# Graph attention: subtracting the shifts and taking the exponentials in three operations a block in place of five

## The chip, the cores and the metric

The kernel runs on one core of one Trainium2 chip. Times are device microseconds (us) of one execution of the whole program; the time before is the median of three runs. The engines are named as the profile names them: PE (TensorE, with PEld for its weight loads), DVE (VectorE), ACT (ScalarE), POOL (GpSimd) and SP (SyncE, which here only issues DMAs).

## The reference, cut to what matters

Four graph layers stand one behind the other, each behind a layer norm and with a residual. The change touches only the last, an attention over edges in which every edge has its own 16 x 16 weights for the message and for the score:

```python
w_m = (efeat @ W_msg + b_msg).reshape(E, in_f, -1)
w_a = (efeat @ W_attn + b_attn).reshape(E, in_f, -1)
h_src = feat[src][:, :, None]
e1 = w_m * h_src
e2 = w_a * h_src
seg_max = jax.ops.segment_max(e2, dst, num_segments=N)
ex = jnp.exp(e2 - seg_max[dst])
denom = jax.ops.segment_sum(ex, dst, num_segments=N)
attn = ex / denom[dst]
ft = jax.ops.segment_sum(e1 * attn, dst, num_segments=N)
return ft.sum(axis=1)
```

There are 3125 nodes and 103125 edges (sorted by their target). In the kernel a running shift, which is at least as large as the scores that it covers, stands for `seg_max`.

## The kernel before, in words

The function `attention_edges` walks over the edges in 44 blocks. A block has 5 groups, and a group has 4 slots of 128 edges (one edge a partition). For each slot a tile `e[:, slot, :]` of 128 x 512 float32 holds the 256 scores e2 and the 256 messages e1 of each edge, in alternating runs of 16. Two blocks are in flight, in the two buffers `e0` and `e1` (index `u`, the other one is `w` or `1 - u`).

For a block, PE multiplies the edge features by the weights (L1724, `product`, tile `wps` in PSUM). What it makes is multiplied by the features of the source node, `hs`, which POOL gathers (L1700, 20 gathers a block). Twelve slots are multiplied by DVE, in three operations of four slots (L1830, the calls `next_block(0)`, `(1)` and `(2)`), and eight by ACT, with 16 small operations a slot (L1793): slots 4, 5, 6 before the exponentials (EARLY), slot 7 behind them (LATE1), and slots 12 to 15 last (LATE3). Then DVE takes maxima over the slots (L1850 and L1852, `largest`, in two steps; the second covers groups 3 and 4 and waits for ACT's last slot), carries them along the five groups (L1859, `up`, and L1864, `down`), makes `scale` (L1881, `rescale`), and subtracts the shift of each group from its scores (L1877, `subtract`). ACT takes the exponential of `scale` (L1799) and of the scores of each group (L1803, `exponentials`). One block later DVE multiplies the messages by the exponentials (L1895, `weigh`), and PE sums the four slots of groups 0 to 3 (L1746, `summed`, tile `slot_sums`); group 4 is summed on DVE (L1904 and L1909). DVE adds the sums up along the groups (L1930 for group 0, L1932 for the others, `accumulate`).

The order on each engine is the order in which the code is written; semaphores stand between the engines, and no scheduler moves anything. On DVE the order of a block around the change is, in `block_step`: `rescale`, `subtract` of group 4, `next_block(0)` (the first of the three multiplications of the next block), `subtract` of groups 3, 2, 1, 0, `accumulate` of group 2, `next_block(1)`, and so on. On ACT it is: EARLY of the next block, the exponential of `scale`, those of groups 4, 3, 2, 1, 0, LATE1 and LATE3 of the next block. Each exponential waits for its own subtraction on the semaphore `a_sub`. PE may refill the four PSUM banks that DVE reads once DVE's multiplication has read them (`a_read_v`), so its products of slots 8 to 11 wait for `next_block(0)`, and those of slots 16 to 19 for `next_block(1)`. ACT has two banks of its own.

Of the kernel before, what the change touches and what calls it, by code (L numbers as in the profile page):

```python
# [106 lines left out]
def bc(ap, axis, n):  # L107

    shape = list(ap.shape)
    shape.insert(axis, n)  # L110
    return ap.unsqueeze(axis).broadcast_to(shape)
# [1470 lines left out]
def attention_edges(nc, io, keep, d, sem, marks, lastrow):  # L1582
# [17 lines left out]
    SUM_READ = (3, 4, 6, 7)  # L1600
    SUM_DONE = (2, 2, 3, 4)
    NM = 2
    assert BG == 5 and SLOTS == 4 and sorted(ORDER) == list(range(BLK))
    with ExitStack() as ctx:
        def sb(name, shape, dt=F32):
# [43 lines left out]
        with nc.Block() as block:  # L1649
# [134 lines left out]
            @block.scalar  # L1784
            def _(act):
                def multiply(u, b, steps):

                    for s in steps:
                        act.wait_ge(a_mult, b * BLK + made(s))
                        bank = VBANKS + BYACT.index(s) % 2  # L1790
                        for f in range(F):
                            at = slice(f * 2 * F, (f + 1) * 2 * F)
                            ins = nc.scalar.mul(e[u][:, s, at], wps[:, bank, at], hs[u][:, s, f:f + 1])  # L1793
                        ins.then_inc(a_read_s, 1)

                def exponentials(u, b):

                    act.wait_ge(a_sub, b * (BG + 1) + 1)
                    nc.scalar.activation(scale[u][:, :], scale[u][:, :], ACT.Exp).then_inc(a_exp, 1)  # L1799
                    for n, g in enumerate(reversed(range(BG))):  # L1800
                        act.wait_ge(a_sub, b * (BG + 1) + (n + 2))
                        e2 = all_e2(u, g, g + 1)[:, 0, :, :]
                        nc.scalar.activation(e2, e2, ACT.Exp).then_inc(a_exp, 1)  # L1803

                act.sem_inc(a_read_s, NS)
                act.wait_ge(a_gather[0], GM)
                multiply(0, 0, BYACT)

                def turn(u, b, gathered):
                    act.wait_ge(a_gather[1 - u], gathered)  # L1810
                    act.wait_ge(a_sum, b * BYPE + 1)
                    multiply(1 - u, b + 1, EARLY)
                    exponentials(u, b)
                    multiply(1 - u, b + 1, LATE1)
                    act.wait_ge(a_sum, b * BYPE + 4)
                    multiply(1 - u, b + 1, LATE3)

                with act.Fori(0, BLOCKS // 2 - 1) as i:
                    turn(0, i * 2, i * GM + GM)
                    turn(1, i * 2 + 1, i * GM + 2 * GM)  # L1820
                turn(0, BLOCKS - 2, BLOCKS // 2 * GM)
                exponentials(1, BLOCKS - 1)

            @block.vector
            def _(dve):
# [45 lines left out]
                    down(u, 1).then_inc(a_shift, 1)  # L1871
                    dve.wait_ge(a_shift, b + 1)

                def subtract(u, g):
                    e2 = e[u][:, g * SLOTS:(g + 1) * SLOTS, :].rearrange("p c (i a o) -> p c i a o", a=2, o=F)[
                        :, :, :, 0, :]
                    nc.vector.tensor_tensor(e2, e2, bc(shift(u, g), 1, SLOTS), ALU.subtract).then_inc(a_sub, 1)  # L1877

                def rescale(u):

# [8 lines left out]

                def weigh(v, u, b):  # L1890

                    dve.wait_ge(a_exp, (b + 1) * (BG + 1))
                    for g in range(BG):
                        pair = e[u][:, g * SLOTS:(g + 1) * SLOTS, :].rearrange("p c (i a o) -> p (c i) a o", a=2, o=F)
                        ins = nc.vector.tensor_tensor(pair[:, :, 1, :], pair[:, :, 0, :], pair[:, :, 1, :], ALU.mult)  # L1895
# [59 lines left out]
                    v.wait(up(v, 0, g))  # L1955
                downs(v, 0, 0)
                rescale(0)
                for g in reversed(range(BG)):
                    subtract(0, g)
                dve.wait_ge(a_gather[1], GM)  # L1960
                for n in range(NV):
                    multiply(1, 1, n)
# [1 line left out]
                def block_step(v, u, b, i, more=True):  # L1964
# [32 lines left out]
                        if more:  # L1997
                            multiply(w, b + 1, n)

                    subtract(u, 4)  # L2000
                    next_block(0)
                    for g in reversed(range(4)):
                        subtract(u, g)
                    accumulate(v, w, b - 1, 2)
                    next_block(1)
                    dve.wait_ge(a_halved, b + 1)
# [258 lines left out]
```

## Time and profile before

| | |
|---|---|
| median of 3 runs | 3073.29 us (3070.06 to 3075.64) |
| profiled execution | 3085.54 us, its span 3083.7 us |
| granted TensorE clock, mean over the span | 0.81 of full speed |
| busy share of the span | PE 74%, DVE 71%, ACT 56%, POOL 46% |
| DVE in the attention stage (1500 to 2900 us) | 1315.67 of 1400 us |
| L1877, subtractions | 220 operations of 128 x 1024, 1215 ns each |
| L1803, exponentials | 220 operations of 128 x 1024, 1107 ns each (median 1057) |

The page gives shares over the whole program. The attention stage is its second half, from about 1390 to 2990 us, and everything that follows is read from that stage: the timeline of each engine through two or three neighbouring blocks, and the groups of instructions and waits in the window from 1500 to 2900 us, which holds 40 of the 44 blocks. In a timeline row the first number is the start, the second the time from the start of the first to the end of the last instruction of the row, and what stands in square brackets is the idle time before it with what ended it.

### The profile page before, as it was taken

Reading aid. Unit: us, or ns where it says so; the run is one execution under the profiler, and the core shown is the slowest. Engines: PE = TensorE matmul, PEld = TensorE weight load, DVE = VectorE, ACT = ScalarE, POOL = GpSimd, SP = SyncE. Lnnn points to the kernel's source line nnn. Section 1 sums busy time; section 2 is a strip of 40 time slices with the busy share of each in tenths; the row PEclk is TensorE's granted clock in tenths of the full one; section 3 lists DMA queues with packets and bytes.
Section 4 is the critical chain, followed back from the end, with each engine's and each line's share of the span. In section 5 each row is a group of like instructions: output and inputs, shape, how many; then the busy total and the mean of one; then the engine's idle time right before and its main releaser. Section 6 shows DMA issues by size and latency. Waiting matters only on the chain. (4 is left out here: it accounts for less than half of the span.)

```text
span 3083.7 us, 36754 instructions
## 1 busy us (share of the span) xinstructions
PE 2284.5 (74%) x7875; PEld 981.3 (32%) x7876; DVE 2192.9 (71%) x3603; ACT 1740.0 (56%) x6804; POOL 1427.2 (46%) x1214
## 2 busy tenths in 40 slices
PE   0588887169755898844888888888888888888860
PEld 0244444024432454321222222332223222223320
DVE  7799996011332444114999999999999999999976
ACT  3377774000110111106888888888888888888833
POOL 6000002710357100025677777677776777777503
PEclk9699999578766899965788888888877888888885
DMA  2000001300254554110222222222222222222113
GB/s 61 7 0 0 0 0 27 107 25 1 73 181 145 145 170 145 60 20 17 69 65 73 65 73 74 69 65 73 65 82 69 65 73 65 82 69 65 65 68 91
DMA packets 122611, 205.66 MB, mean 67 GB/s; under 512 B 55749, under 2 KB 77142, under 8 KB 116574
## 3 DMA queue, kind: packets, MB, share of 16 engines
q1 hardware_dynamic: 81806, 165.79, 15.4%
q0 software_dynamic: 40656, 38.45, 6.6%
q14 instruction: 124, 1.02, 0.1%
q8 instruction: 25, 0.41, 0.1%
HBM read 75.99 MB, written 128.17 MB: 66 GB/s over the span
## 5 line engine op out<-in xcount | busy, mean ns | idle before, releaser
L1700 POOL DMA_INDIRECT hs<-h_table,gix x880 | 1103.4, 1254 | 454.7 <-issue 271.8
L1793 ACT ACTIVATE e<-wps,hs 128x32 f32<-128x32 f32 x5632 | 1034.1, 404 | 239.7 <-PE wps L1724 146.7
L1724 PE MATMUL wps<-w_edge,ef 18*128 18x512 f32 x1760 | 578.8, 708 | 314.6 <-ACT e L1793 152.7
L1746 PE MATMUL slot_sums<-e,ident 128*128 128x512 f32 x1408 | 766.2, 695 | 9.4 <-DVE e L1895 7.0
L1746 PEld LDWEIGHTS slot_sums<-e,ident 128*128 128x128 f32 x1408 | 298.9, 224 | 495.8 <-issue 468.3
L537 POOL DMA_INDIRECT got<-in_edge_rows,start x152 | 153.9, 1013 | 507.9 <-POOLq L449 420.1
L1724 PEld LDWEIGHTS wps<-w_edge,ef 18*128 18x128 f32 x1760 | 159.0, 200 | 691.1 <-ACT e L1793 302.4
L511 ACT CAST edges<-acc 128x400 f32 x600 | 295.4, 492 | 121.0 <-PE acc L498 94.8
L494 PE MATMUL acc<-q_hot,lo_hot 128*128 128x400 bf16 x1200 | 307.0, 338 | 54.4 <-DVE q_hot L468 52.2
L1830 DVE TENSOR_TENSOR e<-wps,hs 128x2048 f32<-128x2048 f32 x132 | 301.5, 2284 | 41.3 <-PE wps L1724 34.2
L468 DVE TENSOR_SCALAR q_hot<-qcol,qT 128x400 bf16<-128x400 bf16 x1200 | 290.3, 316 | 0.9 <-PE acc L498 0.8
L1877 DVE TENSOR_TENSOR e<-e,shifts 128x1024 f32<-128x1024 f32 x220 | 256.6, 1215 | 0.0
L1803 ACT ACTIVATE e<-e 128x1024 f32<-128x1024 f32 x220 | 241.6, 1107 | 25.2 <-issue 9.9
L1895 DVE TENSOR_TENSOR e<-e 128x1024 f32<-128x1024 f32 x220 | 253.4, 1218 | 0.0
L1253 PE MATMUL acc<-edges,msg_parts 128*128 128x448 bf16 x1050 | 225.3, 370 | 36.8 <-DMA msg_parts<-msg 27.9
L498 PE MATMUL acc<-edges,ident_b 128*128 x600 | 202.9, 338 | 0.0
L1281 ACT COPY efT<-tr 128x512 f32<-128x512 f32 x56 | 32.8, 586 | 277.9 <-PE tr L1262 161.4
L494 PEld LDWEIGHTS acc<-q_hot,lo_hot 128*128 128x128 bf16 x1200 | 130.9, 140 | 94.2 <-DVE q_hot L468 69.1
L1850 DVE TENSOR_TENSOR pairs<-e 128x1536 f32<-128x1536 f32 x88 | 130.9, 1488 | 31.0 <-ACT e L1793 30.9
L1253 PEld LDWEIGHTS acc<-edges,msg_parts 128*128 128x128 bf16 x1050 | 106.8, 102 | 134.3 <-DMA msg_parts<-msg 28.3
L829 ACT ACTIVATE agg<-acc 128x448 f32<-128x448 f32 (+1 forms) x15 | 7.4, 535 | 239.1 <-remote 130.3
L1302 DVE SCALAR_TENSOR_TENSOR src_order<-missing,got_order 128x16 int32 (+1 forms) x56 | 10.4, 185 | 175.5 <-DMA got_order<-edges_order 166.2
(362 smaller groups left out, 2167.2 us busy)
## 6 DMA issues: line engine op xcount, KB each, us to landing
rows_state<-states SPq DMA_DIRECT2D x44, 1280.0 KB
rows_shift<-shifts SPq DMA_DIRECT2D x44, 640.0 KB
got_order<-edges_order SPq DMA_DIRECT2D x56, 256.0 KB
ef_order<-efT SPq DMA_DIRECT2D x56, 256.0 KB
ef<-ef_order SPq DMA_DIRECT2D x44, 320.0 KB, 3.0
hs<-h_table,gix POOLq DMA_INDIRECT x880
edges_order<-got SPq DMA_DIRECT2D x38, 256.0 KB
msg<-m_parts SPq DMA_DIRECT2D x10, 480.0 KB
```

Of the source, the lines that this page charges most:

```text
L468: ins = nc.vector.tensor_scalar(q_hot[:, k % HOTS, s, :], qcol[:, :], qT[:, s, at], None, ALU.is_equal)
L494: nc.tensor.matmul(total, lo_hot[:, k // HOTS % 2, :, k % HOTS * 2 + s], q_hot[:, k % HOTS, s, :], start=(s == 0), stop=False)
L511: nc.scalar.copy(edges[:, :, bass.ds(s16, W)], acc[:, k % BANKS, 0:QW].rearrange("p (t w) -> p t w", w=W)).then_inc(taken, 1)
L1253: ins = nc.tensor.matmul(acc[:, at, 0:CW], parts[:, f, k, a, :], edges[:, k, at * CW:(at + 1) * CW], start=(n == 0), stop=(n == 3 * TILES ...
L1700: nc.gpsimd.indirect_dma_start(out=hs[u][:, s, :], out_offset=None, in_=d["h_table"], in_offset=bass.IndirectOffsetOnAxis(ap=gix[u][:, s:s ...
L1724: nc.tensor.matmul(wps[:, bank, :], ef[u][k:k + KM, g * P:(g + 1) * P], w[k:k + KM, :], start=True, stop=True).then_inc(a_mult, 1)
L1746: ins = nc.tensor.matmul(sums[:, g % 2, :], ident[:, :], e[u][:, g * SLOTS + c, :], start=(c == 0), stop=(c == SLOTS - 1))
L1793: ins = nc.scalar.mul(e[u][:, s, at], wps[:, bank, at], hs[u][:, s, f:f + 1])
L1803: nc.scalar.activation(e2, e2, ACT.Exp).then_inc(a_exp, 1)
L1830: nc.vector.tensor_tensor(e[u][:, s0:s1, :].rearrange("p s (i c) -> p (s i) c", c=2 * F), wps[:, 0:s1 - s0, :].rearrange("p s (i c) -> p ( ...
L1877: nc.vector.tensor_tensor(e2, e2, bc(shift(u, g), 1, SLOTS), ALU.subtract).then_inc(a_sub, 1)
L1895: ins = nc.vector.tensor_tensor(pair[:, :, 1, :], pair[:, :, 0, :], pair[:, :, 1, :], ALU.mult)
```

## The change

The scores of two groups are handled by one operation, where before each group had its own: groups 3 and 4, then groups 1 and 2, then group 0 alone. This holds for the subtraction on DVE and for the exponential on ACT. `next_block(0)` keeps its place behind the first subtraction, so it now stands behind that of groups 3 and 4. The semaphores count 4 steps a block in place of 6.

```diff
+    SPANS = ((3, 5), (1, 3), (0, 1))
+    NE = len(SPANS) + 1
...
-                    act.wait_ge(a_sub, b * (BG + 1) + 1)
+                    act.wait_ge(a_sub, b * NE + 1)
                     nc.scalar.activation(scale[u][:, :], scale[u][:, :], ACT.Exp).then_inc(a_exp, 1)
-                    for n, g in enumerate(reversed(range(BG))):
-                        act.wait_ge(a_sub, b * (BG + 1) + (n + 2))
-                        e2 = all_e2(u, g, g + 1)[:, 0, :, :]
+                    for n, (g0, g1) in enumerate(SPANS):
+                        act.wait_ge(a_sub, b * NE + (n + 2))
+                        e2 = all_e2(u, g0, g1)
                         nc.scalar.activation(e2, e2, ACT.Exp).then_inc(a_exp, 1)
...
-                def subtract(u, g):
-                    e2 = e[u][:, g * SLOTS:(g + 1) * SLOTS, :].rearrange("p c (i a o) -> p c i a o", a=2, o=F)[
-                        :, :, :, 0, :]
-                    nc.vector.tensor_tensor(e2, e2, bc(shift(u, g), 1, SLOTS), ALU.subtract).then_inc(a_sub, 1)
+                def subtract(u, g0, g1):
+                    e2 = e[u][:, g0 * SLOTS:g1 * SLOTS, :].rearrange(
+                        "p (g c) (i a o) -> p g c i a o", c=SLOTS, a=2, o=F)[:, :, :, :, 0, :]
+                    low = shifts[u][:, g0:g1, :].rearrange("p g (i o) -> p g i o", o=F)
+                    nc.vector.tensor_tensor(e2, e2, bc(low, 2, SLOTS), ALU.subtract).then_inc(a_sub, 1)
...
-                    dve.wait_ge(a_exp, (b + 1) * (BG + 1))
+                    dve.wait_ge(a_exp, (b + 1) * NE)
...
-                    subtract(u, 4)
+                    subtract(u, *SPANS[0])
                     next_block(0)
-                    for g in reversed(range(4)):
-                        subtract(u, g)
+                    for g0, g1 in SPANS[1:]:
+                        subtract(u, g0, g1)
                     accumulate(v, w, b - 1, 2)
                     next_block(1)
```

On DVE, in the loop, the stretch from `rescale` to `next_block(1)` stood so before (`e0` is the block whose scores are shifted, `e1` the next one; a row with "x4" is four instructions, 128x64x16 is one group's 1024 scores):

```order
L1881 SCALAR_TENSOR_TENSOR scale0<-shifts1,mk0,shifts0 128x256
L1994 ISA
L1877 TENSOR_TENSOR e0<-e0,shifts0 128x64x16
L1829 ISA
L1830 TENSOR_TENSOR e1<-wps,hs1 128x2048
L1877 TENSOR_TENSOR e0<-e0,shifts0 128x64x16 x4
L1924 REGISTER_ALU
L1928 REGISTER_ALU
L1932 SCALAR_TENSOR_TENSOR states1<-states1,mk1,slot_sums 128x512
L1829 REGISTER_ALU
L1830 TENSOR_TENSOR e1<-wps,hs1 128x2048
```

The same stretch of DVE with the change:

```order
L1884 SCALAR_TENSOR_TENSOR scale0<-shifts1,mk0,shifts0 128x256
L1997 ISA
L1880 TENSOR_TENSOR e0<-e0,shifts0 128x128x16
L1831 ISA
L1832 TENSOR_TENSOR e1<-wps,hs1 128x2048
L1880 TENSOR_TENSOR e0<-e0,shifts0 128x128x16
L1880 TENSOR_TENSOR e0<-e0,shifts0 128x64x16
L1927 REGISTER_ALU
L1931 REGISTER_ALU
L1935 SCALAR_TENSOR_TENSOR states1<-states1,mk1,slot_sums 128x512
L1831 REGISTER_ALU
L1832 TENSOR_TENSOR e1<-wps,hs1 128x2048
```

The multiplication of the next block stands behind two groups' subtraction in place of one group's, and the operation behind it covers two groups before it counts its semaphore.

On ACT, in the loop, the exponentials with the change (the last 16 multiplications of EARLY ahead of them, LATE1 behind; `e1` is shifted here, `e0` is the next block):

```order
L1795 ACTIVATE e0<-wps,hs0 128x32 x16
L1801 ACTIVATE scale1<-scale1 128x256
L1803 REGISTER_ALU
L1805 ACTIVATE e1<-e1 128x128x16
L1803 REGISTER_ALU
L1805 ACTIVATE e1<-e1 128x128x16
L1803 REGISTER_ALU
L1805 ACTIVATE e1<-e1 128x64x16
L1791 REGISTER_ALU
L1795 ACTIVATE e0<-wps,hs0 128x32 x16
```

Before, five rows `L1803 ACTIVATE e1<-e1 128x64x16` stood in the place of these three; nothing else moved on ACT, and PE, POOL and SP have the same instructions as before.

## Rows read from the trace of the kernel before

**Rows 1.** The page: busy tenths of DVE in 40 slices of the span.

```profile
DVE  7799996011332444114999999999999999999976
```

**Rows 2.** Groups by form, 1500 to 2900 us: xcount, busy us, mean ns, idle, releasers.

```profile
L1877 DVE TENSOR_TENSOR e<-e,shifts 128x1024 f32<-128x1024 f32 x200 | 233.4, 1215 | 0.0
L1803 ACT ACTIVATE e<-e 128x1024 f32<-128x1024 f32 x199 | 219.0, 1101 | 22.7 <-issue 9.5 <-DVE e L1877 3.7
L1850 DVE TENSOR_TENSOR pairs<-e 128x1024 f32<-128x1024 f32 x40 | 49.0, 1225 | 23.2 <-ACT e L1793 23.2
```

**Rows 3.** Timeline of DVE, blocks from 2000 to 2082 us.

```profile
2000.37 1.23 DVE L1850 TENSOR_TENSOR pairs<-e 128x1024 f32<-128x1024 f32 x1 [0.77 <-ACT e L1793]
...
2006.57 0.69 DVE L1930 TENSOR_TENSOR states<-states,slot_sums 128x512 f32<-128x512 f32 x1 [0.16 <-PE slot_sums L1746]
...
2010.45 1.21 DVE L1877 TENSOR_TENSOR e<-e,shifts 128x1024 f32<-128x1024 f32 x1
2011.59 2.28 DVE L1830 TENSOR_TENSOR e<-wps,hs 128x2048 f32<-128x2048 f32 x1
2013.79 4.62 DVE L1877 TENSOR_TENSOR e<-e,shifts 128x1024 f32<-128x1024 f32 x4
...
2021.78 0.74 DVE L1932 SCALAR_TENSOR_TENSOR states<-states,mk,slot_sums 128x512 f32<-128x512 f32 x1
...
2034.75 1.23 DVE L1850 TENSOR_TENSOR pairs<-e 128x1024 f32<-128x1024 f32 x1 [0.54 <-ACT e L1793]
...
2042.61 0.69 DVE L1930 TENSOR_TENSOR states<-states,slot_sums 128x512 f32<-128x512 f32 x1 [1.83 <-PE slot_sums L1746]
...
2057.81 0.74 DVE L1932 SCALAR_TENSOR_TENSOR states<-states,mk,slot_sums 128x512 f32<-128x512 f32 x1
```

**Rows 4.** Timeline of ACT, the same stretch.

```profile
2013.38 1.31 ACT L1803 ACTIVATE e<-e 128x1024 f32<-128x1024 f32 x1
2015.03 4.46 ACT L1803 ACTIVATE e<-e 128x1024 f32<-128x1024 f32 x4 [0.34 <-issue]
2019.40 7.23 ACT L1793 ACTIVATE e<-wps,hs 128x32 f32<-128x32 f32 x40
...
2027.65 7.07 ACT L1793 ACTIVATE e<-wps,hs 128x32 f32<-128x32 f32 x39 [0.42 <-issue]
```

**Rows 5.** Line L1803: ns min/median/max; timeline of ACT, the first block's exponentials.

```profile
L1803 ACT ACTIVATE e<-e x220: 1052/1057/1439, 1446.4 to 2967.4; 128x1024 f32<-128x1024 f32 x110
...
1446.40 5.22 ACT L1803 ACTIVATE e<-e 128x1024 f32<-128x1024 f32 x5
```

**Rows 6.** The page, groups: two ACT copies of 400 and 512 columns.

```profile
L511 ACT CAST edges<-acc 128x400 f32 x600 | 295.4, 492 | 121.0 <-PE acc L498 94.8
L1281 ACT COPY efT<-tr 128x512 f32<-128x512 f32 x56 | 32.8, 586 | 277.9 <-PE tr L1262 161.4
```

**Rows 7.** Timeline of PE, the same blocks as rows 3.

```profile
2013.92 1.14 PE L1724 MATMUL wps<-w_edge,ef 18*128 18x512 f32 x8 [0.78 <-issue]
2014.99 3.70 PE L1746 MATMUL slot_sums<-e,ident 128*128 128x512 f32 x8
...
2021.32 2.20 PE L1724 MATMUL wps<-w_edge,ef 18*128 18x512 f32 x10 [1.58 <-DVE e L1830]
...
2051.12 5.25 PE L1746 MATMUL slot_sums<-e,ident 128*128 128x512 f32 x8
```

**Rows 8.** Waits, 1500 to 2900 us: total us, times, longest.

```profile
POOL hs L1700 <- ACT e L1793: 161.4, 40, 5.8
DVE states L1930 <- PE slot_sums L1746: 34.2, 32, 2.0
DVE states L1930 <- DVE shifts L1859: 6.7, 8, 1.0
```

**Rows 9.** Stretches: length, busy us of PE, PEld, DVE, ACT, POOL, PEclk, DMA, GB/s.

```profile
2000.40:2006.60 6.20, 6.20 (x18) 2.25 (x20) 5.90 (x10) 4.25 (x17) 4.50 (x4) 1.00 0.07 6
2020.00:2034.70 14.70, 9.73 (x18) 3.11 (x19) 14.01 (x14) 13.97 (x78) 10.15 (x8) 0.62 0.36 117
```

More of the change, by code:

```diff
@@ L1957, in _ @@
                 rescale(0)
-                for g in reversed(range(BG)):
-                    subtract(0, g)
+                for g0, g1 in SPANS:
+                    subtract(0, g0, g1)
                 dve.wait_ge(a_gather[1], GM)
```

## The prediction

> **What bounds the kernel now.** I read the page first. Over the span no engine is full, but DVE's slices show a 9 in nearly every slice of the second half, the attention stage [rows 1]. The chain that ended last reaches back only some 50 us, into the output stage, and says nothing of the blocks. So I took the groups by form for 40 blocks, and then the timelines of DVE, ACT and PE through neighbouring blocks.
>
> The reader is to see that each block is closed by a ring through two engines. The second maximum, L1850, starts at 2000.37 and again at 2034.75 [rows 3]: 34.38 us. Take it apart:
> - from the maximum at 2000.37 to the first subtraction at 2010.45: 10.08 us of DVE work [rows 3];
> - from there to the second exponential at 2015.03: 4.58 us. Between them DVE does that subtraction, the multiplication of the next block and the second subtraction, which begins at 2013.79 and lasts 1.215 us [rows 2, 3], so it ends at 2015.00, and ACT starts 0.03 later. The profile calls ACT's 0.34 us of idle there "issue" [rows 4], but the times show what ended it;
> - from 2015.03 to the next multiplication on ACT at 2019.40: 4.37 us [rows 4];
> - from there ACT multiplies five slots, to 2027.65 + 7.07 = 2034.72: 15.32 us [rows 4];
> - 0.03 us to the maximum, which had waited 0.54 us for just this [rows 3].
>
> The sum is 34.38. Two waits tell that the ring holds everywhere: the second maximum waited for ACT 23.2 us in 40 blocks, 0.58 each [rows 2], and the exponentials stood idle 22.7 us in those blocks, 0.57 each, of which 0.34 is the case above. So what is done on DVE ahead of the second exponential is on the ring, and what DVE does behind it is not: it ends 0.58 us early. DVE's high share is no bound by itself.
>
> One more thing is to be seen in the four exponentials in a row. They take 4.46 us, 1.057 being the last one's own (the median of all [rows 5]), so they start (4.46 - 1.057)/3 = 1.135 us apart [rows 4]. The four subtractions take 4.62 us, which gives (4.62 - 1.215)/3 = 1.135 as well [rows 3]. ACT is paced by DVE. Left alone it is quicker: in the first block, where the subtractions had a lead, five exponentials take 5.22 us, about (5.22 - 1.43)/4 = 0.947 apart, if one record there, which overlaps what was ahead of it, is about as long as the longest of the line, 1.439 [rows 5]; at 5.22/5 each they are 1.044, still under 1.135.
>
> **The change part by part.**
>
> DVE. A subtraction of 1024 scores takes 1.215 us and the next starts after 1.135. One of 2048 has no row; the multiplication of 128 x 2048 lasts 2.28 us and the instruction behind it starts 2.20 us after it (2011.59 to 2013.79) [rows 3]. It reads PSUM and this one does not, so I bound it by the 1024 scores themselves: at most two of them back to back, 1.135 + 1.215 = 2.35, the next start after 2.27; at the other end 0.09 less than the row of 2048, 2.19 and 2.11, should it save twice as much against the two as that row does (0.07). I take the row of the same size, 2.28 and 2.20. A block saves 5 x 1.135 - (2 x 2.20 + 1.135) = 0.14 us on DVE. By itself this is worth nothing: it falls in the part that ends 0.58 us early.
>
> Now the order. Start from the first subtraction, 2010.45. With the change it covers groups 3 and 4, and the multiplication starts at 2012.65 (before 2011.59), the second subtraction, of groups 1 and 2, at 2014.85 and ends at 2014.85 + 2.28 = 2017.13. Before, ACT had its second piece of work at 2015.00. It now has more in its first piece, but not enough.
>
> ACT. What 1024 more columns cost in one exponential: two copies of 400 and 512 columns give (586 - 492)/112 = 0.84 ns a column [rows 6], 0.86 us. The other end is a whole further exponential as the first block spaces them, 0.947 us. I take 0.86, since the fixed part is paid once: 1.057 + 0.86 = 1.91 us. The first exponential starts at 2013.38 as before (it waits for ACT's own EARLY work, not for DVE: the subtraction is done at 2010.45 + 2.28 = 2012.73) and ends at 2013.38 + 1.31 + 0.86 = 2015.55. Then ACT waits for the second subtraction until 2017.16, that is 1.6 us in place of 0.34. The second exponential ends at 2019.07, the third (its scores are subtracted by 2017.05 + 1.215 = 2018.27, so it waits for nothing) 0.947 later, at 2020.02. Before, the last one ended at 2015.03 + 4.46 = 2019.49. So the five slots behind it start **0.53 us later**, and with them the next maximum. Bounds of this term: 0.35 (the subtraction at its lower end, 0.09 off both operations ahead of the second exponential) to 0.95 (both at their upper end, 0.14 on top, the exponential at 2.00, another 0.09, and the last one after 1.135 in place of 0.947, 0.19).
>
> What else moves. `next_block(0)` ends 1.06 us later, so PE's products of slots 8 to 11 start at 2014.98 in place of 2013.92, and the sums of group 3 behind them end at 2019.75 in place of 2018.69 [rows 7]. DVE needs them at 2021.78 [rows 3], ACT for slot 12 at about 2020.0 + 2.9 (a fifth of 15.3, roughly). In the neighbouring block the same sums took 5.25 us, to 2056.37 [rows 7]; 1.06 later is 2057.43, and DVE asks at 2057.81 - 0.14 = 2057.67. Covered, barely; and what is beyond it first eats DVE's lead, which grows to 0.58 + 0.53 + 0.14 = 1.25 us. If that cover were gone too, each us over costs one. `next_block(1)` comes 0.14 earlier. The weighing of the block waits for all exponentials, and stands some 5 us behind them on DVE. POOL's gathers wait for ACT's last slots, 161.4/40 = 4.0 us a block [rows 8], so they have room in a longer block. SP's queue and the DMAs are untouched.
>
> The sum. 42 blocks have the ring as drawn (44 less the first, whose exponentials start late behind ACT's own work and wait for nothing, and the last, which has no next block): 42 x 0.53 = 22.3 us. The first block gains perhaps 0.2, the last 0.1. Together **+22 us**. The profiled execution took 3085.5 us (span 3083.7), so one like it would take 3107.5. The median of the runs is 3073.3, 12 less; the difference is added to it: **3095 us**.
>
> **The rivals.**
>
> A. *Fewer fixed costs win.* The Trainium skill, "VectorE: DVE Perf Modes", section "The TRN2 errata — SBUF-src ops pay a fixed extra latency per instruction", says that a single large tile pays that latency once and many small ones pay it each time. The trace agrees as far as it shows a price (two spacings of 1.135 against one of 2.20 are 0.07 us apart), but has it in a place with slack. As a mechanism in rows: if the second exponential were not held, ACT would be through at 2015.55 + 1.80 + 0.947 = 2018.3, 1.2 us earlier than now, and DVE's lead of 0.58 + 0.14 = 0.72 would be the next limit: 42 x 0.72 = 30 us, 3043 us. For it speaks only that both engines save work; against it that the second subtraction would have to end at 2015.55 and not at 2017.13.
>
> B. *The clock of PE takes more.* DVE waits for the slot sums at L1930: 0.16 us in one block and 1.83 in the next [rows 3], (34.2 + 6.7)/40 = 1.02 on average [rows 8], and this wait is on the ring. The stretch ahead of it, in which PE makes single products and waits, has a granted clock of 0.62, a mixture of both levels (1.2 and 2.4 GHz), and where the clock is back at 1.00 the wait is the short one [rows 9]. The change makes the idle time ahead of slots 8 to 11 longer, 0.78 + 1.06 = 1.84 us, and the wait of PE for ACT behind slots 16 to 19 too. If this brought 1.83 us in each block: 42 x 0.81 = 34 us on top, 3129; half of it, 3112.
>
> The Trainium skill, "TensorE: Matmul & The Clock Gate", section "What's actually happening", has it that activity releases the throttle and the throttled state is the default. That is rival B's direction; no row here shows how a moved gap would be taken.
>
> C. *The clock of PE gives it back*, the side of no loss. The gap of 1.58 us ahead of slots 16 to 19 [rows 7] shrinks to about 1.58 - 1.06 - 0.14 = 0.4, so the sparse stretch that pulls the clock down begins later. If the fall came so late, or ended so early, that every block had the wait of 0.16, the ring would lose 0.86 a block, 36 us: 3095 - 36 = 3059. It decides from a gain of 0.53 a block, that is, once the mean wait falls from 1.02 to 0.5; half of it is 3077.
>
> D. *The change does less than it says*: operations of two groups that cost as much as two. Both engines would then save nothing, with the upper bound of the ring's term: 42 x 0.95 = 40 us, 3113.
>
> **How the numbers follow.** The forecast with its own range (0.35 to 0.7 a block and a wait within 0.2 of today's, 3080 to 3111): 0.60. A: 0.05. B: 0.17. C: 0.13. D: 0.05. About 0.2% (6 us) is what a measurement of this kernel can tell from no change. Faster than 3067: A and the far half of C, 0.08. Within: the near half of C and the lower edge of the forecast, 0.11. Slower than 3079: 0.81. The range to hold 8 in 10 leaves out A, the far half of C and the far half of B: 3072 to 3124.
>
> **What would show it.** In the profile after: the second exponential of a block starts 6.7 us behind the first subtraction, with 1.6 us of idle ahead of it; operations of 2.28 us on DVE and 1.91 us on ACT; the last exponential ends 9.57 us behind the first subtraction (9.04 before); DVE's wait ahead of the second maximum grows from 0.58 to some 1.25; L1930's wait is still near 1.0 (this decides between B, C and the forecast); a block like the one from 2000.37 to 2034.75 takes 34.9 us in place of 34.38. The forecast is wrong if the ring is not one: if DVE did not wait for ACT's last slot, or if the exponentials had no idle time before the second.

## The result, and the profile after

The change made the kernel slower by 3.0%: 3168.55 us, median of 6 runs (3162.42 to 3178.57), against 3077.89 for the kernel before on the same chip, a ratio of 1.0303 (95% interval 1.028 to 1.0326). The forecast was 3095, with a range of 3072 to 3124. Its direction was right, and its size a quarter of the truth: +22 us forecast, +91 us measured. The profiled execution took 3176.3 us with a span of 3174.5 us (before: 3083.7), so it can stand for the others; its mean granted clock is 0.817, as before (0.814).

All of it lies in the blocks. From the page after, the tenths of DVE, which answer to [rows 1], and those of the clock:

```profile
DVE  6899994021332451118898898888888898888876
PEclk9999998587876999757787887778887788788785
```

Where the row of before had a 9 in nearly every slice of the second half, there are now mostly 8s: DVE waits more. Groups by form, 1500 to 2960 us (busy us, mean ns | idle us ahead and its cause), which answer to [rows 2]:

```profile
L1880 DVE TENSOR_TENSOR e<-e,shifts 128x2048 f32<-128x2048 f32 x78 | 177.9, 2280 | 0.0
L1805 ACT ACTIVATE e<-e 128x2048 f32<-128x2048 f32 x78 | 158.4, 2031 | 64.2 <-DVE e L1880 64.2
L1852 DVE TENSOR_TENSOR pairs<-e 128x1024 f32<-128x1024 f32 x39 | 47.8, 1225 | 107.2 <-ACT e L1795 107.2
```

The wait ahead of the second exponential is there, 64.2/39 = 1.6 us a block. But the second maximum now waits 107.2/39 = 2.7 us for ACT, where 0.58 was the measured value before and 1.25 the forecast. Something holds ACT in its five slots behind the exponentials. Waits, 1500 to 2900 us (total us, times, longest), beside [rows 8]:

```profile
ACT e L1795 <- issue: 87.3, 176, 1.3
DVE states L1933 <- PE slot_sums L1748: 24.0, 28, 1.9
```

L1933 is the wait that was L1930 before. It has gone down from 34.2 us, not up. And ACT has 87.3 us of idle in its multiplications that no semaphore explains ("issue"). The same row in the trace of before:

```profile
ACT e L1793 <- issue: 26.8, 78, 0.5
```

To see where the time went I took each block apart at three points: M, the start of the second maximum; R, the start of the small rescaling right ahead of the first subtraction; and the end of the last exponential. All are starts and ends in the timelines; the values are means over 40 blocks, the third to the forty-second. "Low" is the time of a block in which the granted clock was under 1, "sums" the start and end of group 3's sums on PE behind R, "13 to 14" the time between the starts of these slots on ACT.

| kernel | block | M to R | R to last exp | five slots | low | sums | 13 to 14 |
|---|---|---|---|---|---|---|---|
| before | 35.25 | 10.53 | 9.45 | 15.28 | 12.5 | 4.99 to 9.19 | 4.03 |
| after | 37.62 | 10.24 | 9.98 | 17.40 | 14.8 | 6.33 to 11.62 | 5.63 |

The block is 2.37 us longer, and 40 x 2.37 = 95 us against 90.8 in the span. The forecast's term is the third column of times, R to the last exponential: +0.53. The next one, the five slots, carries the miss: +2.12 us, for work that is the same as before; 1.60 of it lies between the starts of slots 13 and 14.

Here are three blocks in a row, beginning (R) at 2038.44, 2073.24 and 2112.70. DVE, which answers to [rows 3]:

```profile
2028.15 1.22 DVE L1852 TENSOR_TENSOR pairs<-e 128x1024 f32<-128x1024 f32 x1 [1.64 <-ACT e L1795]
...
2038.84 2.28 DVE L1880 TENSOR_TENSOR e<-e,shifts 128x2048 f32<-128x2048 f32 x1
2041.04 2.28 DVE L1832 TENSOR_TENSOR e<-wps,hs 128x2048 f32<-128x2048 f32 x1
...
2053.97 5.76 DVE L1898 TENSOR_TENSOR e<-e 128x1024 f32<-128x1024 f32 x5
...
2063.82 1.23 DVE L1852 TENSOR_TENSOR pairs<-e 128x1024 f32<-128x1024 f32 x1 [1.36 <-ACT e L1795]
...
2089.06 5.79 DVE L1898 TENSOR_TENSOR e<-e 128x1024 f32<-128x1024 f32 x5
...
2101.62 1.23 DVE L1852 TENSOR_TENSOR pairs<-e 128x1024 f32<-128x1024 f32 x1 [4.04 <-ACT e L1795]
```

ACT, which answers to [rows 4]:

```profile
2045.56 2.86 ACT L1805 ACTIVATE e<-e 128x2048 f32<-128x2048 f32 x2 [1.64 <-DVE e L1880]
2048.32 6.49 ACT L1795 ACTIVATE e<-wps,hs 128x32 f32<-128x32 f32 x36
...
2083.13 6.35 ACT L1795 ACTIVATE e<-wps,hs 128x32 f32<-128x32 f32 x35
2089.94 0.29 ACT L1795 ACTIVATE e<-wps,hs 128x32 f32<-128x32 f32 x1 [0.46 <-issue]
2090.65 0.29 ACT L1795 ACTIVATE e<-wps,hs 128x32 f32<-128x32 f32 x1 [0.43 <-issue]
...
2093.49 0.47 ACT L1795 ACTIVATE e<-wps,hs 128x32 f32<-128x32 f32 x2 [1.11 <-issue]
...
2122.60 2.94 ACT L1795 ACTIVATE e<-wps,hs 128x32 f32<-128x32 f32 x16
2126.71 3.66 ACT L1795 ACTIVATE e<-wps,hs 128x32 f32<-128x32 f32 x20 [1.18 <-issue]
```

PE, which answers to [rows 7] (a matmul of the program is two instructions there, so the four products and the four sums have x8), and three stretches with their granted clock (the number behind POOL's), which answer to [rows 9]:

```profile
2043.38 1.14 PE L1726 MATMUL wps<-w_edge,ef 18*128 18x512 f32 x8 [1.84 <-DVE e L1832]
2044.45 3.70 PE L1748 MATMUL slot_sums<-e,ident 128*128 128x512 f32 x8
...
2078.19 1.14 PE L1726 MATMUL wps<-w_edge,ef 18*128 18x512 f32 x8 [1.93 <-DVE e L1832]
2079.26 5.40 PE L1748 MATMUL slot_sums<-e,ident 128*128 128x512 f32 x8
2084.59 2.65 PE L1726 MATMUL wps<-w_edge,ef 18*128 18x512 f32 x12
...
2117.66 2.09 PE L1726 MATMUL wps<-w_edge,ef 18*128 18x512 f32 x8 [1.84 <-DVE e L1832]
2119.68 5.95 PE L1748 MATMUL slot_sums<-e,ident 128*128 128x512 f32 x8
```

```profile
2044.40:2048.10 3.70, 3.70 (x13) 1.46 (x9) 3.70 (x4) 2.54 (x2) 3.09 (x3) 1.00 0.02 2
2079.20:2084.60 5.40, 5.40 (x14) 2.05 (x10) 5.40 (x5) 4.24 (x11) 4.49 (x4) 0.68 0.05 5
2119.60:2125.50 5.90, 5.90 (x12) 2.30 (x8) 4.80 (x5) 5.66 (x18) 4.68 (x5) 0.61 0.05 6
```

Read them together:

- In the first block all goes as the forecast had it. The second exponential starts at 2045.56, 6.72 us behind the first subtraction, with 1.64 us of idle; it and the third end at 2048.42, 9.58 us behind (forecast 9.57). The five slots take 2063.82 - 2048.42 = 15.40 us. PE stood idle 1.84 us for `next_block(0)` (0.78 before), but its clock held: 3.70 us for the sums.
- In the second and the third the clock is at its lower level for some 64% and 78% of the four sums (granted clocks of 0.68 and 0.61): they take 5.40 and 5.95 us. The four products ahead of them take 1.14 or 2.09 us.
- What follows is of two kinds. In the third block ACT, through with slot 7 at 2125.54, waits 1.18 us for slot 12, whose product is behind the sums. In the second the products of slots 16 to 19 come late, and `next_block(2)` and the weighing with them: the weighing starts at R + 15.82 (2089.06) against R + 15.53 (2053.97) in the first. And ACT then gets its multiplications slowly: from 2089.94 they start 0.72 us apart, where sixteen in a row take 2.94 us, 0.18 apart. This block lost some 3 us that way; its wait ahead of the second maximum is 4.04 us.

Of the 40 blocks, 6 are like the first (sums of 3.70 us, five slots of 15.42 on average), 21 like the second (5.40 and 17.76) and 13 like the third (5.70 to 6.03, and 17.72). A slow clock in these sums was no loss by itself: the kernel before has sums of 5.06 to 5.29 us in 13 of its 40 blocks, and the five slots take 15.25 us there. But they start at R + 5.07 on average and end by R + 10.4, where those of the second kind end at R + 11.4.

So what the forecast had left out seems to be the clock, but at another place and by another path than its rival B had it. The experiments test this.

### The profile page after: what moved, and what is told of

It reads as the page before. It is cut to its first block and busy times, and to the rows that moved or that the text cites. A ratio compares the mean times of both kernels' runs of the same rounds, so it can differ in the third digit from the quotient of the medians.

```text
span 3174.5 us, 36410 instructions
## 1 busy us (share of the span) xinstructions
PE 2277.0 (72%) x7875; PEld 988.7 (31%) x7876; DVE 2189.6 (69%) x3515; ACT 1726.8 (54%) x6716; POOL 1431.3 (45%) x1214
## 3 DMA queue, kind: packets, MB, share of 16 engines
q1 hardware_dynamic: 81806, 165.79, 14.8%
q14 instruction: 124, 1.02, 0.1%
## 5 line engine op out<-in xcount | busy, mean ns | idle before, releaser
L1726 PE MATMUL wps<-w_edge,ef 18*128 18x512 f32 x1760 | 547.3, 724 | 406.8 <-ACT e L1795 128.5
L1748 PE MATMUL slot_sums<-e,ident 128*128 128x512 f32 x1408 | 804.3, 725 | 9.4 <-DVE e L1898 6.8
L1748 PEld LDWEIGHTS slot_sums<-e,ident 128*128 128x128 f32 x1408 | 311.9, 233 | 530.6 <-issue 493.4
L1805 ACT ACTIVATE e<-e 128x2048 f32<-128x2048 f32 x132 | 220.1, 1704 | 71.5 <-DVE e L1880 71.5
L1880 DVE TENSOR_TENSOR e<-e,shifts 128x2048 f32<-128x2048 f32 x132 | 250.5, 1926 | 0.0
L1302 DVE SCALAR_TENSOR_TENSOR src_order<-missing,got_order 128x16 int32 (+1 forms) x56 | 10.4, 186 | 176.1 <-DMA got_order<-edges_order 169.0
```

Source lines behind the costliest of these rows:

```text
L1726: nc.tensor.matmul(wps[:, bank, :], ef[u][k:k + KM, g * P:(g + 1) * P], w[k:k + KM, :], start=True, stop=True).then_inc(a_mult, 1)
L1748: ins = nc.tensor.matmul(sums[:, g % 2, :], ident[:, :], e[u][:, g * SLOTS + c, :], start=(c == 0), stop=(c == SLOTS - 1))
L1880: nc.vector.tensor_tensor(e2, e2, bc(low, 2, SLOTS), ALU.subtract).then_inc(a_sub, 1)
```

## The experiments

Every time is a median, and its ratio is against runs of the kernel before taken beside it. That kernel's own median went from 3074 to 3081 us between sets, so a few us between two experiments of different sets say nothing. "Means" are those of the table above.

### Which part of the change costs it

The first set took the change apart: the multiplication behind two subtractions, with all operations one group each (e1); the exponentials alone in pairs (e2); the subtractions alone in pairs (e4). A fourth kernel asked whether the store of the states holds ACT back.

e1, the order alone, from the kernel before:

```
+                    subtract(u, 3)
                     next_block(0)
-                    for g in reversed(range(4)):
+                    for g in reversed(range(3)):
                         subtract(u, g)
```

> Five subtractions and five exponentials as before; only next_block(0) stands one subtraction later (behind groups 4 and 3), so it ends 1.13 us later, about as much as the changed kernel has it (1.06). Measured in the changed kernel: last exponential +0.53 us, the five slots behind it 15.28 -> 17.40 us a block (+2.1). Theory P (the late multiplication, through PE's products of slots 8 to 11 and the sums behind them, makes the +2.1): about 2 us a block more than before, 3078 + 85 = 3160 us. Theory S (the +2.1 is a stretch in which ACT and PE get their instructions slowly, which starts some 1.8 us behind the start of the state store and lasts longer when ACT's slots come 0.5 us later; the late multiplication has no part in it): the last exponential is still paced by the subtractions and ends where it did, 3078 to 3085 us.

Measured: 3170.15 us, ratio 1.0291 (1.0228 to 1.0353). The last exponential ends where it did before (9.45 us behind R), and no operation is wider, and yet a loss of the same size is here. The block is 37.53 us: the five slots take 16.89 us, M to R 11.19. The path is not quite that of the change. All 40 blocks of e1 are of the third kind (sums of 5.91 to 5.99 us): slot 12 starts 4.71 us behind slot 7, 2.72 before, and from slot 13 to 14 it is 3.68 us, with no slow stretch.

e2, the exponentials alone, from the kernel before:

```
-                    for n, g in enumerate(reversed(range(BG))):
-                        act.wait_ge(a_sub, b * (BG + 1) + (n + 2))
-                        e2 = all_e2(u, g, g + 1)[:, 0, :, :]
+                    for g0, g1 in ((3, 5), (1, 3), (0, 1)):
+                        act.wait_ge(a_sub, b * (BG + 1) + (BG + 1 - g0))
+                        e2 = all_e2(u, g0, g1)
...
```

> Exponentials over two groups at a time, subtractions one by one with next_block(0) in its old place. The second exponential has to wait for the third and fourth... by the spacing of 1.135 us the first (groups 3, 4) starts at 4.58 us behind the first subtraction, the second at 6.85, the last ends at 9.7 (9.04 before): +0.65 us a block on the ring, and PE is not delayed. Theory P: only that, 3078 + 27 = 3105 us, ACT's five slots still 15.3 us. Theory S: ACT's slots come 0.65 later, the slow stretch grows as in the changed kernel, 15.3 -> about 17, 3165 us.

Measured: 3104.46 us, ratio 1.01 (1.0061 to 1.014). The multiplication stands where it stood, and only the ring's term is left: the last exponential ends at R + 10.13 (9.45), the five slots take 15.33 us as before, the block 35.81.

e4, the subtractions in pairs, the exponentials one by one, from the kernel after:

```
-                    for n, (g0, g1) in enumerate(SPANS):
+                    for g, n in ((4, 0), (3, 0), (2, 1), (1, 1), (0, 2)):
...
-                        e2 = all_e2(u, g0, g1)
+                        e2 = all_e2(u, g, g + 1)
...
```

> Subtractions over two groups at a time with next_block(0) behind the first of them, exponentials one by one. Last exponential: the one of group 2 starts at 6.71 us behind the first subtraction, then two more at 0.947: ends at 9.66, +0.62 us a block. Both theories give about what the changed kernel takes, 3165 to 3175 us; if the length of the exponentials had a part in the slow stretch, it would differ.

Measured: 3174.99 us, ratio 1.0323 (1.0283 to 1.0364), a block of 37.71 us. Taking the exponentials apart again gives nothing back.

e5, the store of the states half a block later, from the kernel after:

```
+                        store_states(u, i * 2 + (u - 2))
...
-                        store_states(1 - u, i * 2 + (u - 1))
...
```

> The changed kernel with the store of a block's states (1280 KB) issued some 8 us later, behind the load of the next features, away from ACT's slots 12 to 15. Theory S: the slow stretch moves or goes, ACT's five slots fall towards 5 x 2.72 = 13.6 to 15.3 us, 3100 us or less. Theory P, and any theory in which the store has no part: unchanged, 3168 us.

Measured: 3145.38 us, ratio 1.0241 (1.0201 to 1.0281). Neither theory had this. The stretches of slow multiplications are there with no store beside them, so the store is not what makes them. It gave some 22 us back, measured against the kernel before of either set (the five slots take 16.48 us in place of 17.40), by what path stays open.

So the loss beyond the ring's term goes with the one thing that e1, e4 and the change share: `next_block(0)` a microsecond later.

### Is it the idle time of PE

e7 takes group 3's sums out of the way: they go ahead of the products that wait for `next_block(0)`.

```
+                    add(3)
                     for_dve(u, b, 1, NV + 1)
-                    add(3)
                     for_act(u, b, (12,))
```

e8 leaves the order, and fills PE's idle time ahead of these products with two matmuls whose result is thrown away:

```
+                    if before is not None:
+                        pe.wait_ge(a_weighed, before * BYPE + 4)
+                        pe.wait_ge(a_acc, before * BG + SUM_READ[3])
+                        for _ in range(2):
+                            nc.tensor.matmul(sums[:, 1, :], ident[:, :], e[u][:, 3 * SLOTS, :],
+                                             start=True, stop=True)
                     for_dve(u, b, 1, NV + 1)
```

> The changed kernel, but PE sums group 3 ahead of the products of slots 8 to 11, so it has 3.7 us of work while it would wait for next_block(0). In the changed kernel PE idles 1.84 us there (0.78 before), and the four products (2.09 us, 1.14 before) and the sums behind them (5.4 to 6 us, 3.7 before) run at the lower clock in most blocks. Theory C (the gap pulls the clock down, and what is late by it is the cost): sums of group 3 end near 5.8 us behind the scaling in each block, ACT's five slots fall back to 15.3 us, only the ring's 0.53 us a block is left, 3078 + 22 = 3100 us. Theory S (slow issue on ACT from its later place): ACT's slots stay at 17 us, 3165 us.

> The changed kernel with two more matmuls of 128 x 512 (about 0.93 us each at the higher clock) ahead of the wait for next_block(0); they write the bank that the sums of group 3 overwrite afterwards, and nothing else is moved. Theory C: PE has no gap, the clock stays up, the late products cost nothing by themselves, 3100 us. If the mere lateness by 1.06 us of the products and sums (and not the clock) is the cost, nothing changes, 3168 us.

Measured: e7 3081.68 us, ratio 1.0023 (1.0009 to 1.0038); e8 3096.3 us, ratio 1.0068 (1.0043 to 1.0093). e8 is the plainest of all tests: the same products, sums and operations as in the change, 1.98 us of extra work on PE, and 72 us less. Timeline of PE in e8:

```profile
2019.50 1.98 PE L1771 MATMUL slot_sums<-e,ident 128*128 128x512 f32 x4
2021.42 1.14 PE L1726 MATMUL wps<-w_edge,ef 18*128 18x512 f32 x8
2022.49 3.70 PE L1748 MATMUL slot_sums<-e,ident 128*128 128x512 f32 x8
```

There is no idle time ahead of the four products, and the sums take 3.70 us, in this block as in all 40. They still start at R + 6.03, so their later start alone costs nothing. The block is 35.67 us with five slots of 15.34, and the rest over the kernel before is the ring's: +0.42 a block, x 42 = 18 us. Against the kernel before of its own set (3075.5) e8 takes 21 us more; the forecast had 22. In e7 the sums run in the time in which PE had been idle (timeline of PE; waits of ACT):

```profile
2034.93 3.70 PE L1748 MATMUL slot_sums<-e,ident 128*128 128x512 f32 x8
2038.56 1.98 PE L1726 MATMUL wps<-w_edge,ef 18*128 18x512 f32 x10
```

```profile
ACT e L1795 <- issue: 12.4, 47, 0.4
```

It also shows that the amount of low clock does not tell the cost: e7 has as much of it as the change (14.8 us a block), but not over the sums of group 3, which take 3.70 us in all 40 blocks. ACT's unexplained idle falls from 87.3 to 12.4 us. That e7 even wins back most of the ring's 0.53 (its five slots take 15.00 us, 0.28 less than before, and M to R 10.26) I had not expected.

e9 is the control: the same edit as e7 on the kernel before.

> The kernel before with the same order on PE (sums of group 3 ahead of the products of slots 8 to 11), as a control for the two above. Theory C: the gap before was 0.78 us and pulled the clock down in one block of three at most, so little is to be had: 3065 to 3080 us. If the order alone is worth 2 us a block, it shows here too: below 3030 us.

Measured: 3077.67 us, ratio 1.0005 (0.9988 to 1.0023), nothing. In the kernel before, where PE idles 0.78 us, the order of these sums does not matter.

### Can the change be made to win

e10 is e7 with all three subtractions ahead of `next_block(0)`, so that no exponential waits.

```
-                    subtract(u, *SPANS[0])
-                    next_block(0)
-                    for g0, g1 in SPANS[1:]:
+                    for g0, g1 in SPANS:
                         subtract(u, g0, g1)
+                    next_block(0)
```

> Pairs of groups as in the changed kernel, but all three subtractions stand ahead of next_block(0), with the sums of group 3 first on PE. By the ring: exponentials start 2.93 us behind the first subtraction and are no longer held: 1.91 + 1.80 + 0.95, the last one ends at about 7.6 (9.04 before, 9.57 in the changed kernel), 1.4 us a block less than before; DVE's own work allows some 0.7 to 1.2 of it. 3078 - 42 x 0.9 = 3040 us, bounds 3010 and 3060. next_block(1) will wait some 0.5 us for PE's products of slots 8 to 11, and if this late next_block(0) pulls the clock down where it is needed, the gain is lost: 3100 us or more.

Measured: 3169.76 us, ratio 1.0312 (1.0283 to 1.0342), a miss of 130 us. The last exponential ends 1.23 us earlier than before (R + 8.22), where 1.4 was expected, and that is lost three times over: the five slots take 19.2 us. ACT, PE and DVE in one block of e10:

```profile
2019.68 6.04 ACT L1795 ACTIVATE e<-wps,hs 128x32 f32<-128x32 f32 x32
...
2029.87 2.60 ACT L1795 ACTIVATE e<-wps,hs 128x32 f32<-128x32 f32 x14 [4.15 <-PE wps L1726]
```

```profile
2023.76 3.79 PE L1726 MATMUL wps<-w_edge,ef 18*128 18x512 f32 x10 [1.65 <-issue]
2027.70 2.07 PE L1726 MATMUL wps<-w_edge,ef 18*128 18x512 f32 x2 [0.15 <-remote]
```

```profile
2027.70 2.29 DVE L1832 TENSOR_TENSOR e<-wps,hs 128x2048 f32<-128x2048 f32 x1 [1.95 <-PE wps L1726]
```

ACT, through with slots 7 and 12 at 2025.72, waits 4.15 us for slot 13. Its product stands on PE behind those of slots 16 to 19, which must wait until `next_block(1)` has read their banks, and the five run at the lower clock (3.79 us; five such products take 1.98 at the higher). I had looked at ACT's wait and not at what is queued ahead of it. This explains 1.8 us of the 4.15: by its row, whose end the profile models, the product of slot 13 is done at 2027.55, and ACT starts at 2029.87. DVE's `next_block(2)` also starts late, at 2027.70, where the products of slots 16 to 19 end at 2025.85 by their rows; over the blocks this difference is 1.8 us on average. What holds both up is not shown.

e11 fills PE's sparse stretch in the kernel before: one throw-away matmul ahead of the products of 16 to 19, two ahead of slot 14, one ahead of slot 15.

```
...
+                def fill(before, n):
+                    if before is None:
+                        return
+                    pe.wait_ge(a_acc, before * BG + (BG + 3))
+                    for _ in range(n):
+                        nc.tensor.matmul(sums[:, 0, :], ident[:, :], bc(ones[:, :], 1, 4), start=True, stop=True)
...
+                    fill(before, 1)
                     for_dve(u, b, 2, NV + 2)
-                    for_act(u, b, (13, 14, 15))
+                    for_act(u, b, (13,))
+                    fill(before, 2)
+                    for_act(u, b, (14,))
+                    fill(before, 1)
+                    for_act(u, b, (15,))
```

> The kernel before with matmuls on constants, whose results nobody reads, in the three places where PE waits late in a block: one ahead of the products of slots 16 to 19, two ahead of slot 14, one ahead of slot 15 (0.93 us each at the higher clock). Theory C (PE's waits late in a block pull the clock down over the sums of groups 1 and 0, and the wait at L1930, 1.02 us a block on average, is its price): the clock stays up, the wait falls to 0.2 and ACT's first slots come earlier, 3076 - 42 x 0.8 = 3042 us. If the clock falls all the same, the added work at half speed delays slots 14 and 15: 3090 us or more.

Measured: 3066.36 us, ratio 0.9946 (0.9923 to 0.9969): faster than both kernels, but by 15 us against the kernel before beside it (3081.47), less than half of the 34 expected. The low time of a block falls from 12.5 to 4.9 us, the mean clock rises from 0.814 to 0.866, and DVE's wait for the sums ahead of the rescaling nearly goes (waits of e11; before, 34.2 us in 32):

```profile
DVE states L1942 <- PE slot_sums L1746: 6.8, 5, 1.5
```

M to R is 0.93 us shorter; 0.24 of it is given back in the five slots (15.52), so the block is 34.57.

e12 puts both together, e7 and these fillers.

> The changed kernel with the sums of group 3 ahead of slots 8 to 11 (3082 us alone) and the same added matmuls. Theory C: the same gain as in the kernel before, 3082 - 34 = 3048 us; it stays behind the kernel before with added matmuls, since the ring's 0.53 us a block is still there.

Measured: 3142.44 us, ratio 1.0198 (1.0177 to 1.0219), a miss. With the sums ahead PE has less to do behind `next_block(0)`. In the block shown it idles 1.07 us ahead of the products of slots 16 to 19, these and that of slot 13 run at the lower clock, and so do the two fillers ahead of slot 14 behind them. Timeline of PE in e12 and, for the same two matmuls, in e11:

```profile
2038.77 3.82 PE L1726 MATMUL wps<-w_edge,ef 18*128 18x512 f32 x10 [1.07 <-DVE e L1844]
2042.51 3.68 PE L1757 MATMUL slot_sums<-ones,ident 128*128 128x512 f32 x4
```

```profile
2046.27 1.98 PE L1755 MATMUL slot_sums<-ones,ident 128*128 128x512 f32 x4
```

At 3.68 in place of 1.98 us they are in the way: slots 13 and 14 start 4.68 us apart (4.27 in e11), and the five slots take 16.44. In e11 the fillers held the clock up; here they met it low and delayed what is queued behind them.

### The slow multiplications

What is left is how a late `next_block(2)` goes with ACT's slow stretch, which makes 1.60 of the 2.12 us. POOL's gathers show a difference too. Timeline of POOL after, over the starts of two weighings (2053.97, a good block, and 2089.06, a stretched one):

```profile
2052.88 0.94 POOL L1702 DMA_INDIRECT hs<-h_table,gix  x1 [0.30 <-issue]
2054.13 1.87 POOL L1702 DMA_INDIRECT hs<-h_table,gix  x1 [0.30 <-DVE e L1832]
...
2088.94 0.94 POOL L1702 DMA_INDIRECT hs<-h_table,gix  x1 [0.30 <-issue]
2090.19 0.94 POOL L1702 DMA_INDIRECT hs<-h_table,gix  x1 [0.30 <-issue]
2091.44 1.96 POOL L1702 DMA_INDIRECT hs<-h_table,gix  x1 [0.30 <-issue]
```

A gather that starts just behind the weighing is held, 1.87 us in place of 0.94. Where one starts just ahead of it, it is not, nor is the next. e13 moves the weighing of the kernel before by three small copies (some 0.3 us) and nothing else; e14 does so to the kernel after.

```
+                    for k in range(3):
+                        v.add(nc.vector.tensor_copy(late[u][:, k, :, :], marks[:, cols(b, BG), :]))
                     weigh(v, w, b - 1)
```

> The kernel before with three copies of 10 columns, which nobody reads, ahead of the weighing on DVE, so that it starts some 0.25 us later (15.68 -> 15.9 us behind the scaling). Open is why ACT gets its multiplications of slot 13 slowly for 1.5 us in most kernels and for 3.5 us in blocks of the changed one. In all traces so far the long stretch comes where the weighing starts at 15.82 and a gather on POOL started ahead of it at 15.70 and was not held; the short one where the gather started just behind the start of the weighing and was held for 1.87 us. Theory W (this order of gather and weighing sets it): here the gather at 15.85 now comes first, ACT's five slots grow from 15.3 to about 17 us, 3150 us. Theory C (only PE's clock matters, the order does nothing): DVE has 0.58 us of lead there, 3076 to 3082 us.

> The changed kernel with the same three copies: the weighing starts at 16.05 in place of 15.82 in most blocks, and the gather at 16.94 falls inside its first operation and is held. Theory W: the long stretch shortens to 1.5 to 2.5 us, 3168 - 40 = 3130 us. Theory C: unchanged, 3168 us.

Measured: e13 3138.36 us, ratio 1.02 (1.0168 to 1.0233). 0.3 us of copies cost 64 us (the kernel before beside it: 3074.07). Timelines of DVE, POOL and ACT in e13:

```profile
2009.95 5.75 DVE L1896 TENSOR_TENSOR e<-e 128x1024 f32<-128x1024 f32 x5
```

```profile
2009.76 0.95 POOL L1701 DMA_INDIRECT hs<-h_table,gix  x1 [0.30 <-issue]
2011.01 0.97 POOL L1701 DMA_INDIRECT hs<-h_table,gix  x1 [0.30 <-issue]
```

```profile
2003.28 7.77 ACT L1794 ACTIVATE e<-wps,hs 128x32 f32<-128x32 f32 x42
2012.18 0.47 ACT L1794 ACTIVATE e<-wps,hs 128x32 f32<-128x32 f32 x2 [1.13 <-issue]
2013.61 0.29 ACT L1794 ACTIVATE e<-wps,hs 128x32 f32<-128x32 f32 x1 [0.96 <-issue]
```

It is the same picture as in the change, in a kernel whose exponentials end at R + 9.45 and whose sums end at R + 9.03, as before: a gather 0.2 us ahead of the weighing, unheld, and multiplications a microsecond apart. The five slots take 17.22 us. So a slow stretch comes without any late sums, from a small shift of the weighing alone.

e14 took 3169.3 us, ratio 1.0317 (1.0289 to 1.0345): no gain, where theory W had 3130 and theory C no change. The five slots did get shorter (17.40 to 16.90), but M to R grew by 0.33 us, and in many blocks the weighing started later still; the block is 37.46 us, 0.16 less than after. It says that the order of the gather and the weighing is not enough to mend it. Nor is that order enough to make it: in 38 of the 40 blocks of e1 a gather starts some 0.3 us ahead of the weighing, which stands at R + 17.3 there, and takes its 0.94 us unheld, and yet slots 13 and 14 are 3.68 us apart. So e13 speaks for theory W, e1 and e14 speak against it as it stands, and what slows ACT stays open.

## Why the prediction was wrong

- **The ring** (10.08 + 4.58 + 4.37 + 15.32): right as a reading of the kernel before, and in what it forecast of the exponentials. Its last term, the five slots, was held fixed, and it grew. The last exponential ends 9.58 us behind the first subtraction, forecast 9.57; the idle time ahead of the second is 1.64, forecast 1.6; the term of 0.53 us a block is 9.98 - 9.45 in the means.
- **Its cost alone, +22 us, 3095**: right for what it covers. With PE's gap filled (e8) the kernel takes 21 us more than the kernel before, and with the exponentials alone in pairs (e2) 28, where 27 was expected.
- **The operations**: 2.28 us on DVE, as taken. So rival D falls. ACT's exponentials of two groups average 2.03 us, and this too is as forecast: in the blocks shown the first takes 2.16 us (1.31 + 0.86 = 2.17 in the sum), the second 1.91.
- **"What else moves"**: this is the step that failed. It moved the products of slots 8 to 11 and the sums behind them by 1.06 us, kept their durations, and called the wait for them "Covered, barely". In the means the sums start 1.34 us later and last 5.29 us in place of 4.20, so that they end 2.43 us later. I had the two rows side by side, 3.70 and 5.25 us for the same four sums [rows 7], and took the longer one as a bound for a neighbouring block only, not as what a longer gap makes of 34 blocks in 40. ACT's slot 12, the products of 16 to 19 and `next_block(2)` all stand behind these sums, and ACT's five slots, which the sum had at 15.32 us, took 17.40. With the sums at 3.70 us again, and no earlier start, they take 15.34 (e8).
- **Rival B** had the right cause (a gap of PE of 1.84 us, named there) and the wrong place. It put the price on DVE's wait at L1930, which fell from 34.2 to 24.0 us, and no more than 34 us in all. The price was in ACT's five slots, 2.12 us a block, of which 2.06 is gone in e8.
- **The weighing** was dismissed with "some 5 us behind them on DVE": true of its inputs, but it is timed by `next_block(2)`, and 0.3 us there cost 64 us in the kernel before (e13). Nothing in the rows of before told that; that DVE and POOL meet there was to be seen in POOL's two lengths of 0.94 and 1.87 us, which I had not looked at.
- **Rival A** was not met in this order of instructions. e10, which built its condition, had the last exponential 7.82 us behind the first subtraction, as in this rival's sum (2018.3 - 2010.45 = 7.85), but 3169.76 us in place of 3043: the time went into ACT's wait for slot 13. **Rival C** did not come: 14.8 us of low clock a block against 12.5.
- **What stays open**: the late sums explain ACT's wait for slot 12 (13 blocks in 40, and all of e1). How they lead to the slow stretch between slots 13 and 14, which is the larger part of the 2.12 us, is not explained: it goes when the sums are fast again (e7, e8), and it can come without them (e13).

## What to carry to other kernels

A step that moves a microsecond later can also make the engine behind it idle for a microsecond more: for PE, look up what the work behind that gap takes at either clock level in the rows you have, and price the change with the long one. Ask then who is queued behind it, not only who reads it. And before an order is given up, try to move the work that needs the fast clock ahead of the gap (e7, 87 us back), or to fill the gap (e8, 72 us). Try them one by one: e7 alone took 6 us more than the kernel before, and together with the fillers of e11 it took 61 us more (e12).

## What the runs showed of the hardware

- A gap of 1.84 to 1.93 us ahead of PE's four products can leave the clock alone (3.70 us of sums, 6 blocks in 40), or come with a fall in the midst of the sums (5.40, 21 blocks) or ahead of them (5.95 in the block shown, 13 blocks of this kind). 1.98 us of matmuls in the gap kept it at 1.00 in the block shown, and the sums at 3.70 us in all 40 (e8).
- The issue of an indirect gather on POOL takes 0.94 us. Where it starts 0.1 to 0.2 us behind the start of one of the weighing's five operations it takes 1.87 us (1.96 at 2091.44), 1.47 where it starts 0.5 to 0.6 us behind, and 0.94 where it starts with the next one, as at 2090.19 (medians over all runs). Each so ends 2.0 to 2.1 us behind the start of that operation.
- During the weighing ACT's small multiplications can come 0.72 us apart, with no semaphore that explains it. How long this lasts changed with 0.3 us of shift of the weighing (e13). I have seen it and moved it, but its cause stays open.
